# Superblock one-hots by four scalar comparisons in a graph and expert layer on one core

## The reference, cut to what matters

```python
h = layernorm(x)
m = clifford_linear(h[src] * relation_emb[edge_type])   # a linear map, so it can follow the sum
m = m * sigmoid(gate(relation_emb[edge_type])) * norm(deg[src], deg[dst])
h_agg = segment_sum(m, dst)                             # edges summed per destination node
x = x + clifford_linear(h + h_agg)
# then, per node: router softmax over 8 experts, each expert
# relu(bn(. @ W1)), relu(bn(. @ W2)), . @ Wo, weighted and added to x
```

## Time and profile before

| what | value |
|---|---|
| median of 3 runs | 1877.46 us (1876.61 to 1878.33) |
| profiled execution, its own time | 1872.02 us |
| its span, first to last instruction | 1869.9 us |
| mean granted TensorE clock | 0.980 |
| busy: PE / DVE / ACT / POOL | 94% / 62% / 70% / 73% of the span |
| DVE line 1295 (the one-hots of the places) | 196 times, 133.6 us |
| POOL line 458 (the gathers) | 1,266 times, 1352.9 us |

### The profile page before, as it was taken

The page is one execution under the profiler, slowest core; times in us unless marked ns, Lnnn a source line. Parts: engine busy times, 40 slices in busy tenths (PEclk is TensorE's granted clock), DMA queues, the critical chain, the costliest instruction groups (busy, mean ns, idle before and its releaser), DMA issues.

```text
span 1869.9 us, 31246 instructions
## 1 busy us (share of the span) xinstructions
PE 1766.2 (94%) x10694; PEld 1602.7 (86%) x10694; DVE 1167.4 (62%) x2407; ACT 1310.4 (70%) x2960; POOL 1371.3 (73%) x1391
## 2 busy tenths in 40 slices
PE   5846889999999999999999999999999999999998
PEld 5835888888989989989989989998998998997888
DVE  8966566656656656656656666756665665665552
ACT  5546777768777767777768767777876776773455
POOL 5867777777777777777777777777777777777720
PEclk9977999999999999999999999999999999999999
DMA  8167344445444434434445435434444443433320
GB/s 252 52 248 229 101 135 133 109 127 136 114 117 133 127 104 131 130 105 132 126 108 135 127 107 132 129 104 129 134 115 117 133 126 105 135 109 106 105 45 6
DMA packets 93691, 231.21 MB, mean 124 GB/s; under 512 B 23338, under 2 KB 44838, under 8 KB 93595
## 3 DMA queue, kind: packets, MB, share of 16 engines
q0 software_dynamic: 60768, 168.61, 34.2%
q1 hardware_dynamic: 32012, 60.45, 10.5%
q10 hardware_dynamic: 815, 1.16, 0.2%
HBM read 216.69 MB, written 13.44 MB: 123 GB/s over the span
## 4 chain that ended last, share of the span: by engine, by line
POOL 57%; PE 19%; issue 18%; DVE 4%; DMA 2%; ACT 1%; DVEq 0%; POOLq 0%; SPq 0%
POOL H L458 36%; POOL R L458 21%; PE z L829 8%; PE y L853 4%; DVE H L1011 2%; PE pr L889 2%; PE y L740 2%; PE o L877 1%; DMA H<-h_table,src 1%; DMA h_table<-big 1%; ACT big L563 1%; PE y L805 0%; PE y L786 0%; DVE acc L1227 0%; DMA src<-in_src 0%
## 5 line engine op out<-in xcount | busy, mean ns | idle before, releaser
L458 POOL DMA_INDIRECT H<-h_table,src x784 | 817.5, 1043 | 248.3 <-issue 238.5
L458 POOL DMA_INDIRECT R<-r_table,typ x482 | 535.4, 1111 | 164.3 <-issue 163.7
L644 ACT ACTIVATE h<-z,bns 128x256 f32<-128x256 f32 (+1 forms) x864 | 418.5, 540 | 325.1 <-PE z L829 323.0
L1227 DVE SCALAR_TENSOR_TENSOR acc<-y,wg,acc 128x256 f32<-128x256 f32 x392 | 173.5, 480 | 476.3 <-PE y L853 475.1
L596 ACT ACTIVATE OH<-tb,iota_t 125x128 fp32r<-125x128 int32 x1208 | 383.7, 392 | 65.1 <-PE pr L889 49.9
L829 PE MATMUL z<-h,big 128*128 128x256 f32 (+1 forms) x1728 | 376.9, 362 | 3.2 <-ACT h L644 2.8
L829 PE MATMUL z<-hT,big 128*128 128x256 f32 (+1 forms) x1728 | 377.3, 362 | 0.7 <-ACT h L644 0.7
L853 PE MATMUL y<-big,h 128*128 128x256 f32 x1568 | 374.4, 380 | 1.7 <-DVE lg L1196 1.6
L889 PE MATMUL pr<-RH,OH 125*128 125x258 f32 x1208 | 334.8, 312 | 26.9 <-DVE H L1286 16.3
L829 PEld LDWEIGHTS z<-h,big 128*128 128x128 f32 x1728 | 306.7, 192 | 39.6 <-ACT h L644 4.4
L853 PEld LDWEIGHTS y<-big,h 128*128 128x128 f32 x1568 | 294.3, 191 | 38.8 <-issue 1.9
(11 more groups left out here) (166 smaller groups left out, 1511.9 us busy)
## 6 DMA issues: line engine op xcount, KB each, us to landing
tb<-in_typ_row SPq DMA_DIRECT2D x24, 728.0 KB
H<-h_table,src POOLq DMA_INDIRECT x784, 2.8
R<-r_table,typ POOLq DMA_INDIRECT x482, 2.8
h_table<-big SPq DMA_DIRECT2D x7, 910.0 KB, 8.6
big<-in_x SPq DMA_DIRECT2D x7, 896.0 KB, 10.9
big<-in_w SPq DMA_DIRECT2D x8, 768.0 KB, 4.8
acc<-in_x SPq DMA_DIRECT2D x22, 256.0 KB, 7.1
hxT<-in_xt SPq DMA_DIRECT2D x22, 256.0 KB
```

Source lines behind the costliest of these rows:

```text
L458: pool.indirect_dma_start(out=to[:, b * DX:(b + 1) * DX], out_offset=None, in_=tab, in_offset=bass.IndirectOffsetOnAxis(ap=ix[:, J * SB + ...
L644: last = s_.activation(o[:, m, 0:wide_], z_[:, m, 0:wide_], ACT.Relu, bias=bns[:, l, 1, c:c + 1], scale=bns[:, l, 0, c:c + 1])
L1227: last = v.scalar_tensor_tensor(out=acc[:, g % 3, t, :], in0=b[:, t * D:(t + 1) * D], scalar=wg[:, t, e_:e_ + 1], in1=acc[:, g % 3, t, :], ...
```

## The change

`places_dve` wrote all 4 x 128 numbers of a superblock in one instruction that compares two tensors, `dloc` (each column repeated 128 times) and `iota_w` (the row repeated 4 times). Now it issues four instructions that each compare the row `iota_w` with one column of `dloc` as a scalar per partition. The values of `S` are the same.

```diff
                     if J > 1:
                         dve.wait_ge(mm, J - 1)
-                    v.tensor_tensor(S[:, J % 2, :, :], dloc[:, J * SB:(J + 1) * SB].unsqueeze(2).to_broadcast([P, SB, P]),
-                                    iota_w[:, 0:P].unsqueeze(1).to_broadcast([P, SB, P]), ALU.is_equal)
+                    for b in range(SB):
+                        v.tensor_scalar(S[:, J % 2, b, :], iota_w[:, 0:P], dloc[:, J * SB + b:J * SB + b + 1], None, ALU.is_equal)
```

## The result

| | before | after |
|---|---|---|
| median, compared on one chip | 1877.03 us (1870.47 to 1878.49, 6 runs) | 1869.34 us (1867.77 to 1869.72, 6 runs) |
| ratio, 95% interval | | 0.9963 (0.9950 to 0.9977) |
| profiled execution, its span | 1869.9 us | 1866.9 us |

The change makes the kernel 0.4% faster, inside the predicted range and 2.3 us over the predicted 1867.0. That closeness flatters the sum, and is in part luck: two of its terms were right, one had the wrong sign and one was three times too small, as the traces show.

A forecast was written before the change was run, and what follows sets the result against it. POOL's gathers were taken as the bound, PE as nearly equal. Terms of -2.8, -2.1, -7.4 and +1.8 us summed to -10.5, taking the median 1877.46 us to 1867.0, range 1859 to 1872.

The forecast's parts named there:

- The form frees POOL: At line 1295's comparison: its 97 gather stalls go, half counted, putting POOL 15 us ahead at 1703 us.
- the rule of the prediction: For POOL's gathers: a held gather ends as if begun 0.12 us before the DVE instruction holding it ended.
- the stalls come back: Rival, chance 0.19: lines 1282 and 1304 hold POOL instead, nearly all 30 us return; 1879 us, or 1874 to 1876.
- The wait near 1,700 us: At 1702.86 us: PE gets back 4.5 us of waiting and 2.9 of slow clock, -7.4 us.
- The early gain of 2.8 us: To 451 us the kernel is POOL's, so PE gains POOL's 2.8 us (0 to -5.6).
- The three longer middle groups: Groups from 696.67, 765.67 and 1379.75 us lose their excess over 68.13 us: -2.1 us.
- DVE's price of a comparison: In each superblock: four new comparisons take 0.79 us against 0.60 for the old one, +0.19 us.
- The rival of one number at a time: Rival, chance 0.12: DVE's new comparisons run slower, costing PE 7.2 us instead of 1.8; 1872.4 us.
- The thin place: Superblock behind the expert weights, once a group: DVE's delay exceeds 0.11 us slack, +1.8 us, 7.2 by the upper price.
- the prediction's own signs: If right: line 1296 near 0.28 us, gathers 10 to 25 us shorter, no late line 796 wait, undisturbed groups 68.2 us.
- The carried 5.4 us: Profiled execution of before stood 5.4 us under the median of its runs; that distance was added to the forecast unchanged.
- The rival that POOL is held harder: Rival, chance 0.09: four comparisons block POOL's SBUF ports longer than one did, 22 us more; 1899 us.

The follow-up runs named there:

- The four tensor against tensor: Changed kernel's four comparisons written as tensor-tensor instructions of 128 numbers; on the second chip 1880.46 us, ratio 1.0050 to the kernel before.
- the second trace of before: The kernel before, unchanged, profiled again on a second chip: 1870.20 us, ratio 1.0001.
- fourth chip: Chip where the kernel before has a median of 1874.98 us; the changed kernel, run again there, took 1869.18 us, ratio 0.9962.
- the repeat of the changed kernel: The changed kernel, unaltered, run again on another chip: 1869.18 us, ratio 0.9962 to the kernel before.
- The run with only the comparison's delay: Changed kernel with line 1210's cast made a tensor-tensor maximum of its operand with itself: 1866.30 us, ratio 0.9981 to the kernel before.
- the third and the fourth experiment: Changed kernel with the old comparison kept behind the expert weights: 1866.04 us; changed kernel with line 1210's cast as a two-operand maximum: 1866.30 us.

## Why the prediction was right, and which terms were not

**The form frees POOL: right, at half the size.** By the rule of the prediction, which puts a held gather down to the instruction whose end frees it, line 1296 holds 13 gathers with 0.9 us in the changed kernel, where line 1295 held 97 with 30.2. Two more begin in line 1296 and are held to the end of the product behind it, with 1.47 and 0.70 us (six, with 5.6 us, began so in line 1295). The four tensor against tensor show that it is the form. But I counted 15 us of POOL's gain at 1,703 us, and the gathers are only 6.5 us shorter. I set all gathers between 125 and 1,790 us against DVE's instructions as in the prediction: line 1304 held 124 with 51.5 us (125 with 60.0 in the second trace of before) and holds 166 with 79.9 now (169 with 80.8 in the second trace), while line 1282 holds 5 us less. Of the 30 us three quarters came back, most of them at line 1304. The rival "the stalls come back" was the better description of POOL; it failed in its consequence, since the quarter that stayed was enough.

**The wait near 1,700 us: right in place and mechanism, and in size for this trace.** -7.4 was forecast, 4.5 of the wait and 2.9 of the clock; -7.0 is measured. The two sides of the sum were off and cancelled. The gather behind the first 1,200 starts at 1689.94, not 1698.76 us, so POOL is 8.8 us ahead there, and PE is 3.6 us late by 1656.8 (1653.2 before). Against PE, POOL is 12.4 us ahead, where I had 11.9 and needed 5.64. All ten traces of the first, second and fourth chip agree on the mechanism: PE waits 4.54, 2.97 and 4.59 us at line 796 there in the three where every comparison is tensor against tensor, and 0.65 us once and not at all six times in the seven with the new form. Against the second trace of before (65.5 us) the same group gives back only 3 us. One reading of the prediction was wrong, without a term that hangs on it: the chain of before doesn't leave POOL for good near 1,400 us, it runs over gathers once more from 1,578 us up to this wait.

**The early gain of 2.8 us: wrong.** The step that failed is "POOL is 1.2 us ahead at 264 us, 2.8 at 451", and -2.8 came out as +0.9. To 451 us all stalls together are 22.6 us before and 23.4 after (26.2 and 24.3 in the two other traces), so POOL is not ahead at all. Of PE's waits the one at 269.37 shrinks, and two ahead of it, which were 5.03 and 3.27 us, grow. PE after:

```profile
171.56 0.55 PE L889 MATMUL pr<-RH,OH 125*128 125x258 f32 x1 [5.91 <-DVE H L1286]
181.11 0.69 PE L796 MATMUL z<-ident,sums 128*128 128x128 f32 x2 [4.73 <-DVEq L1273]
...
268.75 0.65 PE L796 MATMUL z<-ident,sums 128*128 128x128 f32 x4 [1.98 <-DVEq L1273]
```

In the repeat of the changed kernel PE waits 5.31 us at 306.54 instead. The early part cut at the first and third group start, before and then after, shows where it goes:

```profile
0.00:184.31 184.31, 116.79 (x979) 107.05 (x980) 143.16 (x213) 98.51 (x285) 128.07 (x205) 0.86 0.62 197
184.31:353.37 169.06, 150.33 (x985) 138.13 (x985) 104.68 (x224) 130.73 (x307) 130.98 (x126) 0.96 0.44 119
```

```profile
0.00:186.73 186.73, 115.65 (x982) 105.38 (x982) 145.02 (x233) 98.42 (x285) 130.46 (x206) 0.87 0.61 195
186.73:353.85 167.12, 152.00 (x982) 138.53 (x981) 108.99 (x287) 130.35 (x307) 129.35 (x125) 0.95 0.44 120
```

The middle stretch gains 1.9 us, and the first loses 2.4 (185.09 and 186.61 us in the second traces, 186.48 with the four tensor against tensor). Seven superblocks' comparisons fall into that first stretch, 7 x 0.19 = 1.3 us more of DVE by the sum, and PE waits there for DVE's products. The prediction priced DVE's time only in the wide groups. That this is the loss is argued and not tested; the sum of the first 492 us changes by 0.9, less than the 3.3 between two traces of the kernel before.

**The three longer middle groups: right.** All 17 are within 0.15 us of each other now; in before's 1161.0 us the three took 2.0 us more than the thirteen undisturbed ones did (68.17 each), and 2.1 was forecast for it.

**DVE's price of a comparison: right.** 0.78 to 0.79 us for four against 0.60, the forecast +0.19; the mean of line 1296 is 301 ns and its busy time 176.7 us, where 280 and 170 were named as the signs. The rival of one number at a time is dead. The two parts of the price hold too: a row of eight pieces of 64 puts them 0.162 us apart and a row of four of 128 puts them 0.196 apart, so 64 numbers are 0.034 us and 0.13 us is fixed, where the prediction had 0.067 for 128 numbers and 0.13 fixed.

**The thin place: the mis-sized term.** +1.8 us was forecast; the middle groups alone pay 0.29 each over 68.17, 4.9 us for 17 (0.32 over the 68.13 of the second trace, 5.4 us), and some 6 in 20, near my upper bound of 7.2. Three of the prediction's own signs came out against it here and at POOL: groups of 68.45 us and not 68.2, a PE wait of 0.21 us behind `LO` in every group, and gathers 6.5 us shorter and not 10 to 25. Two things are behind it. First, the slack. I took 0.05 us from the earlier trace rows as what PE needs behind `LO` and read a slack of 0.11 from the 0.16 of the earlier trace rows. Where PE really waits at this place, it starts 0.12 behind `LO` (1061.66 and 1061.78), so the slack was 0.04. The run with only the comparison's delay fits: 0.19 less 0.04 is its 0.15. Second, a term that wasn't in the sum at all: the cast, +0.18 us just ahead of the comparisons. By the sum 0.19 + 0.18 - 0.04 = 0.33, against 0.29 to 0.32 measured.

**The carried 5.4 us.** Profiled execution against profiled execution, the change is worth -3.0, not -10.5; median against median -7.7 here and -5.8 on the fourth chip. I carried the distance between the profiled execution of before and its median along unchanged; it is 0.3 us in the changed kernel (1869.01 and 1869.34). This is the luck: the sum was 7.5 us too low, the carried distance 5.1 too high, and 2.3 is left. Before's executions spread over 8 us on the first chip and the fourth and nearly 12 on the second, those of the changed kernel over 2 to 3. The natural reading is that the wait near 1,700 us is what spreads, and that the change removes it in every execution; the second trace of before, with 65.5 us in that group, points to it. Against it stand the third and the fourth experiment, whose traces have no such wait and whose executions still spread over 6.0 and 6.5 us. No trace of one of the slower executions of before was taken, so it stays open how much of the 4.7 us is that wait.

**The rival that POOL is held harder: dead,** by 19 gathers with 1.4 us in the worse of two traces, and one in rows of eight, with 0.06. The Trainium skill's page "SBUF — State Buffer", section "SBUF: two separate sides", says that a DVE instruction with two SBUF inputs contends with a GpSimd instruction that reads SBUF. That half agrees with lines 1282, 1304 and the four tensor against tensor, which hold gathers up to 0.12 us before their own end. Its other half, that GpSimd is locked out by a two-port mode, is not what rows of short comparisons show; the last section has what does wait.

## What to carry to other kernels

Where GpSimd issues indirect gathers one after the other, a DVE instruction with two tensors in SBUF delays them, and one with a scalar per partition doesn't, even if it takes more of DVE; but a stall that is removed at one instruction can return at the longest of the others (28 us more at line 1304 here), so count on it only where a named wait ends. Price DVE time where PE stands close behind DVE, once per group, with the delay from DVE's end to PE's start read at that very place. And compare medians of several executions: one trace on either side was off by more than half the effect here.

## What the runs showed of the hardware that was not expected

The contention goes both ways, by form. The cast of line 1210 (one tensor in SBUF) takes 0.18 us alone. If it still runs in the last part of a gather, it ends when the gather ends: begun 0.55 to 0.57 us behind the gather's start it takes 0.38 to 0.40, begun at 0.61 to 0.63 it takes 0.32 to 0.34, begun at 0.73 to 0.76 it takes 0.19 to 0.23, and each sum is about 0.95, the gather's length. At 0.42 it takes 0.18 and is not held. From before and from the kernel with `LO` in four pieces:

```profile
1055.26 0.95 POOL L458 DMA_INDIRECT H<-h_table,src  x1 [0.30 <-issue]
...
1056.01 0.20 DVE L1210 CAST wg<-wg 128x32 fp32r<-128x32 f32 x1
```

```profile
1056.94 0.95 POOL L458 DMA_INDIRECT H<-h_table,src  x1 [0.30 <-issue]
...
1057.36 0.18 DVE L1210 CAST wg<-wg 128x32 fp32r<-128x32 f32 x1
```

So the change moved the cast within the gathers' beat, from 0.75 us behind a gather's start to 0.56, and cost it 0.11 to 0.18 us in every wide group, without touching it. With two operands the same work at the same point (0.54 to 0.63) takes 0.19 us and doesn't wait. The Trainium skill's page "SBUF — State Buffer", in the same section, says that whichever of the two starts first holds the ports for its whole length; the late part of a gather agrees, while a cast that is begun and over within its first 0.6 us does not.
